# Input statistics on ScalarE, negative scales on GpSimd: a macaron block with two FP4-quantised feed-forward layers

## The chip, the cores and the metric

The kernel runs on one core of one Trainium2 chip. The metric is the device time of one execution in microseconds (us); lower is better. All arithmetic between the engines is synchronised by semaphores that the kernel places by hand, so each engine works through its own list of instructions in a fixed order and stops at a wait until another engine has counted far enough.

## The reference

```python
def _ffn(x):                       # x: (4096, 256); w_gate, w_up: (704, 256); w_down: (256, 704)
    gate = fp4_linear(x, w_gate)   # both operands quantised in blocks of 16 along the last dim
    y = fp4_linear(x, w_up)
    return fp4_linear(silu(gate) * y, w_down)

def fp4_quant_dequant(x):          # per block of 16
    scale = maximum(max(abs(xb)) / 6, 1e-12)
    q = GRID[searchsorted(MID, abs(xb / scale))] * sign(xb / scale) * scale

x = x + 0.5 * _ffn(layernorm(x))
x = x + attention(layernorm(x))    # complex projections, 2 batches of 2048 rows, width 256
x = x + 0.5 * _ffn(layernorm(x))
```

`layernorm` is (x - mean) / sqrt(var + 1e-5) over 256 columns, without gain or bias. Everything is float32.

## The kernel before

The 4096 rows of x are 32 tiles (NT = 32) of 128 rows, kept in on-chip memory as `x[:, t, :]`. Three stages follow each other: the first feed-forward layer (f = 0), attention, and the second feed-forward layer (f = 1). The change touches the two feed-forward stages alone.

A feed-forward stage is a software pipeline written out by hand. Each engine has a function `step(c, par)` and runs it for c up to 33; in step c the engines work on several tiles at once:

- TensorE transposes the quantised row of tile c (eight 128x128 transposes, `bank<-ident,zq`), computes gate and up of tile c + 3 (`gate_up`, in three column parts; the first waits for `gu_read`, that is, until VectorE has read the gate and up of the tile before), and projects tile c down (`bank_b<-wd_hl`).
- ScalarE copies the transposes out (`T_hi`), takes the SiLU of tile c + 3, normalises tile c + 7 into the last 256 columns of `z` (`normalise`, waits `yx_done`), takes absolute values of the scaled row, and copies the down projection out (`down`). In the first stage it also takes the statistics of the new x of tile c - 2 for attention: sum (L1298), minus mean twice (L1304, L1305), variance (L1311).
- VectorE multiplies SiLU by up (`product`, L776), takes the maximum of each block of 16 (`amax`, L787) of one whole row `z` of 960 columns (704 of tile c + 3 in the next step, and 256 normalised columns of a later tile), makes `s_up` (L790), `s_neg` (L794) and the reciprocal `s_inv` (L799), rounds (`rounded`, `grid`), and from tile 4 on makes the low part of the transposes (`T_lo`, L870).
- GpSimd adds the down projection of tile c - 1 to x (`residual`, L544), scales the row of tile c + 2 by `s_inv` (`y`, L552; waits `rnd_done`), and multiplies the grid of tile c + 1 by `s_neg` (`zq`, L568).

`whole(f, k)` is true for the tiles whose row GpSimd scales in one piece: k = 2 to 27 in the first stage, 3 to 27 in the second. For k from 28 on VectorE scales 704 columns itself (`scaled`, L827).

The statistics of the input (mean and variance of the 32 tiles of x as they come in) are made by ScalarE for tiles 0 to 7 ahead of the loop. For tiles 8 to 31 VectorE makes them with `bn_stats` and `bn_aggr`: two tiles in each step with c % 4 == 2, two more in each step with c % 4 == 3, there with four `bn_aggr` and two small operations for the group. Groups 3 to 7 (tiles 12 to 31) fall into steps 2 to 19 of the first stage. `group_std` on GpSimd turns a group's variances into 1/std in each step with c % 4 == 0.

```python
def step(c, par):                                   # VectorE
    blocks_of(c, par)                               # scales(c + 2), to_grid(c + 1), lower(c)
    if f == 0 and c >= 0:
        input_statistics(c)
    if hidden(c + 3):
        product(c + 3)
```

Of the kernel before, what the change touches and what calls it, by code (L numbers as in the profile page):

```python
# [15 lines left out]
SIX = 6.0  # L16
# [14 lines left out]
def macaron_kernel(nc, x_in, wq, bq, wk, bk, wv, bv, wo, bo, w_gate, w_up, w_down, out):  # L31
# [35 lines left out]
    with ctx:  # L67
# [140 lines left out]
        gate_done = sem("gate_done")  # L208
        amax_done, up_done, inv_done = sem("amax_done"), sem("up_done"), sem("inv_done")
        y_done, yx_done, abs_done = sem("y_done"), sem("yx_done"), sem("abs_done")  # L210
        rnd_done, grid_done, zq_done = sem("rnd_done"), sem("grid_done"), sem("zq_done")
# [66 lines left out]
        def wait_scaled(engine, f, k):  # L278

            if hidden(k) and not whole(f, k):  # L280
                engine.wait_ge(y_done, scaled_apart(f, k))
            if ahead(k):
                engine.wait_ge(yx_done, NT * f + k + LEAD + 1)

        def last(k):
# [158 lines left out]
        def _(pool):  # L444
# [22 lines left out]
            def group_std(g):  # L467

                q = slice(4 * g, 4 * g + 4)
                if g < 2:  # L470
                    pool.wait_ge(x_var, 4 * (g + 1))
                    nc.gpsimd.tensor_tensor(out=var[:, q], in0=var[:, q], in1=eps_all[:, q],
                                            op=ALU.add).then_inc(x_eps, 1)
                    pool.wait_ge(x_eps, g + 1)
                else:
                    pool.wait_ge(g_stats, 2 * (g - 1))
                nc.gpsimd.tensor_tensor(out=rstd[:, q], in0=var[:, q], in1=mhalf[:, q],
# [62 lines left out]
            def ffn_step(f):  # L540
                def residual(t, par):
# [3 lines left out]
                                            op=ALU.add).then_inc(x_new, 1)  # L545

                def scaled_by_pool(k):

# [7 lines left out]
                def quantised(k, par):  # L556

                    pool.wait_ge(grid_done, number(f, k))
                    if f or between(k, 1 - LEAD, NT - 1):
                        pool.wait_ge(T_done, number(f, k) - 1)  # L560
# [11 lines left out]

                def step(c, par):
                    if hidden(c - 1) and c < NT:
                        residual(c - 1, 1 - par)
# [115 lines left out]
        def _(dve):  # L691
# [77 lines left out]
            def ffn_step(f):  # L769
# [9 lines left out]
                def scales(k, par):  # L779
# [5 lines left out]
                    if lo == 0:  # L785
                        dve.wait_ge(gu_read, NT * f + k + 1)
                    nc.vector.tensor_reduce(out=amax[:, n], in_=blocks(z[:, lo:hi]), axis=AX_X, op=ALU.max,  # L787
                                            apply_absolute_value=True).then_inc(amax_done, 1)
                    dve.wait_ge(amax_done, number(f, k))
                    nc.vector.scalar_tensor_tensor(out=s_up[:, n], in0=amax[:, n], scalar=TINY * SIX,  # L790
                                                   in1=c_up[:, n], op0=ALU.max, op1=ALU.mult).then_inc(up_done, 1)
                    if f or between(k, 2 - LEAD, NT - 1):
                        dve.wait_ge(zq_done, number(f, k) - 2)
                    nc.vector.scalar_tensor_tensor(out=s_neg[:, par, n], in0=amax[:, n], scalar=TINY * SIX,  # L794
                                                   in1=c_neg[:, n], op0=ALU.max, op1=ALU.mult)
                    dve.wait_ge(up_done, number(f, k))
# [57 lines left out]
                def input_statistics(c):  # L854

                    g = (c + 10) // 4
                    if c % 4 == 2 and g < NT // 4:
                        tile_statistics(4 * g)
                        tile_statistics(4 * g + 1)
                    if c % 4 == 3 and g < NT // 4:  # L860
                        tile_statistics(4 * g + 2)
                        tile_statistics(4 * g + 3)
                        group_statistics(g)

# [41 lines left out]
                def step(c, par):  # L906
                    blocks_of(c, par)
                    if f == 0 and c >= 0:
                        input_statistics(c)
                    if hidden(c + 3):  # L910
# [286 lines left out]
        def _(act):  # L1197
# [90 lines left out]
            def bias_rows():  # L1288
# [3 lines left out]
                nc.scalar.activation(bias_row[:], bv_sum, ACT.Copy).then_inc(aw["rows_s"], 1)  # L1292

            def mean_of(t, n):

                if n:
                    act.wait_ge(stats_done, n)
                nc.scalar.activation(st_junk[:, 0, :], x[:, t, :], ACT.Identity,  # L1298
                                     accum_out=total[:, bass.ds(t, 1)]).then_inc(total_done, 1)
# [49 lines left out]
            def ffn_step(f):  # L1349
# [69 lines left out]
                def step(c, par):  # L1419
                    measured = f == 0 and 0 <= c - 2 < NT - 2  # L1420
                    extra = f == 0
                    if chain(c + 1) and (f or not last(c + 1)) and (f or c != -1):
# [11 lines left out]
                    if measured:  # L1434
                        act.wait_ge(x_new, c - 1)
                        mean_of(c - 2, c - 2)
                    if c < 0:
                        silu_gate(c + 3)
# [8 lines left out]
                    if measured:  # L1447
                        minus_mean(c - 2, c - 2)
                    if c >= 0 and hidden(c + 3):
                        silu_gate(c + 3)  # L1450
# [15 lines left out]
                    if measured:  # L1466
                        variance_of(c - 2, c - 2)
                    if f and 2 <= c < 2 + 2 * QT:
                        new_statistics(NT - 2 * QT + c - 2)
# [807 lines left out]
```

## Time and profile before

| what | value |
|---|---|
| median of 3 runs | 918.5 us (918.35 to 918.93) |
| the profiled execution: its time, its span | 917.84 us, 916.0 us |
| busy share: PE, VectorE (DVE), ScalarE (ACT), GpSimd (POOL) | 97%, 78%, 66%, 58% |
| granted TensorE clock over the span | 1.00 |

Stages by the trace: weights and first tiles to about 49 us, steps 0 to 31 of the first feed-forward layer 49 to 264 us, attention to about 704 us, steps 0 to 31 of the second layer 704 to 916 us. Busy time of a whole stage says little about what ends a wait there: in the two feed-forward stages TensorE and VectorE are both above 93% busy (209.8 and 202.5 of 215.1 us; 204.7 and 201.5 of 212.0 us), in attention TensorE has 438.1 of 440.0 us and VectorE 265.6.

### The profile page before, as it was taken

How to read it: one execution, taken by the hardware profiler on the slowest of the kernel's cores; microseconds unless marked ns; L12 is line 12 of the kernel's file. 1: busy time of each engine (PE TensorE's matmuls, PEld its weight loads, DVE VectorE, ACT ScalarE, POOL GpSimd, SP SyncE). 2: the span in 40 equal slices, each digit the busy share in tenths (PEclk: the TensorE clock that was granted, in tenths of full speed). 3: DMA queues.
4: the chain of work that ended last, by engine and by line, in shares of the span. 5: the costliest groups of instructions: out<-in, count | busy, mean ns of one | idle time of the engine just before them, and what ended most of it. 6: DMA issues, size and time to landing. Idle time of an engine off the chain costs nothing.

```text
span 916.0 us, 16066 instructions
## 1 busy us (share of the span) xinstructions
PE 888.2 (97%) x5608; PEld 796.9 (87%) x5608; DVE 711.8 (78%) x1189; ACT 601.6 (66%) x1263; POOL 528.4 (58%) x562
## 2 busy tenths in 40 slices
PE   4999999999999999999999999999999999999997
PEld 3789889889988898989998898988988899999986
DVE  7979999999976666665573644545599999999998
ACT  6777667767674675758675576767784666555543
POOL 5577778777520254545663154546577667777662
PEclk9999999999999999999999999999999999999999
DMA  9100000000000000000000000000000000000001
GB/s 317 60 1 1 1 1 2 1 1 1 1 2 0 1 2 1 1 1 1 1 1 1 1 1 1 1 1 1 1 1 1 1 25 24 24 24 24 24 1 47
DMA packets 11951, 13.80 MB, mean 15 GB/s; under 512 B 864, under 2 KB 11104, under 8 KB 11872
## 3 DMA queue, kind: packets, MB, share of 16 engines
q1 hardware_dynamic: 11872, 12.79, 4.2%
q8 instruction: 45, 0.74, 0.3%
q14 instruction: 34, 0.28, 0.1%
HBM read 8.59 MB, written 4.19 MB: 14 GB/s over the span
## 4 chain that ended last, share of the span: by engine, by line
PE 64%; DVE 26%; issue 5%; POOL 3%; ACT 1%; DMA 0%; SPq 0%; DVEq 0%; POOLq 0%; ACTq 0%
PE bank L2085 19%; PE bank L1831 12%; PE bank L2123 5%; PE bank L2127 4%; PE bank L2125 4%; DVE amax L787 4%; DVE grid L814 4%; DVE rounded L808 4%; PE bank L1712 4%; DVE z L776 4%; PE bank_b L1842 3%; DVE T_lo L870 3%; PE bank L2048 2%; PE bank_b L1849 2%; POOL p_lo L615 2%
## 5 line engine op out<-in xcount | busy, mean ns | idle before, releaser
L615 POOL TENSOR_TENSOR p_lo<-s_ring,p_hi 128x512 fp32r<-128x512 f32 x128 | 167.4, 1313 | 218.0 <-ACT p_hi L1570 217.9
L982 DVE TENSOR_TENSOR top<-bank,top 128x512 f32<-128x512 f32 x112 | 77.4, 691 | 125.7 <-ACT s_ring L1554 125.7
L1831 PE MATMUL bank<-w_hi,T_hi 128*128 128x512 f32 (+1 forms) x384 | 150.4, 392 | 5.7 <-DVE z L776 5.5
L568 POOL TENSOR_TENSOR zq<-grid,s_neg 128x256 f32<-128x256 f32 (+2 forms) x184 | 141.9, 798 | 17.7 <-DVE grid L814 17.7
L552 POOL TENSOR_TENSOR y<-z,s_inv 128x960 f32<-128x960 f32 (+1 forms) x56 | 98.4, 1757 | 83.8 <-DVE rounded L808 79.0
L1831 PE MATMUL bank<-w_hi,T_lo 128*128 128x512 f32 (+1 forms) x384 | 143.8, 374 | 0.0
L1831 PE MATMUL bank<-w_lo,T_hi 128*128 128x512 f32 (+1 forms) x384 | 143.4, 373 | 0.0
L1382 ACT ACTIVATE T_hi<-bank 128x1024 fp32r<-128x1024 f32 (+1 forms) x68 | 64.6, 951 | 105.1 <-PE bank L1712 105.1
L1554 ACT ACTIVATE s_ring<-bank 128x512 f32<-128x512 f32 x128 | 75.9, 593 | 78.0 <-PE bank L2085 77.9
L2123 PE MATMUL bank<-v_hl,p_hi 128*128 128x258 f32 x384 | 109.9, 286 | 0.4 <-DVE x L1014 0.2
L2127 PE MATMUL bank<-v_hl,p_lo 128*128 128x258 f32 x384 | 108.2, 282 | 0.0
L2125 PE MATMUL bank<-v_hl,p_hi 128*128 128x256 f32 x384 | 108.1, 282 | 0.0
L2085 PE MATMUL bank<-q_hi,k_hi 128*128 128x512 f32 x256 | 101.2, 395 | 0.8
L2085 PE MATMUL bank<-q_lo,k_hi 128*128 128x512 f32 x256 | 100.6, 393 | 0.0
L2085 PE MATMUL bank<-q_hi,k_lo 128*128 128x512 f32 x256 | 100.2, 392 | 0.0
L1560 ACT ACTIVATE s_ring<-s_ring 128x512 f32<-128x512 f32 x128 | 79.2, 622 | 18.5 <-DVE s_ring L1004 18.5
L1831 PEld LDWEIGHTS bank<-w_hi,T_hi 128*128 128x128 f32 x384 | 72.2, 188 | 17.3 <-issue 6.9
L1004 DVE TENSOR_TENSOR s_ring<-s_ring,bank 128x512 f32<-128x512 f32 x128 | 84.8, 678 | 1.3 <-PE bank L1712 0.8
L1570 ACT ACTIVATE p_hi<-s_ring 128x512 fp32r<-128x512 f32 x128 | 80.7, 632 | 7.1 <-PE bank_b L2127 3.5
L1831 PEld LDWEIGHTS bank<-w_hi,T_lo 128*128 128x128 f32 x384 | 72.1, 188 | 10.9
L1842 PE MATMUL bank_b<-wd_hl,T_hi 128*128 128x256 f32 x600 | 80.4, 279 | 0.1
L787 DVE TENSOR_REDUCE amax<-z 128x60 f32<-128x960 f32 (+2 forms) x72 | 74.9, 1040 | 7.0 <-ACT z L1416 2.0
(232 smaller groups left out, 2204.2 us busy)
## 6 DMA issues: line engine op xcount, KB each, us to landing
out<-x SPq DMA_DIRECT2D x7, 512.0 KB, 2.9
x<-in_L_attn_hidden_states SPq DMA_DIRECT2D x3, 1024.0 KB, 12.3
x<-in_L_attn_hidden_states SPq DMA_DIRECT2D x2, 512.0 KB, 6.9
wraw<-in_L_ffn_w_down SPq DMA_DIRECT2D x1, 704.0 KB, 7.3
wraw<-in_L_ffn_w_up SPq DMA_DIRECT2D x1, 640.0 KB, 4.8
wq_s<-in_L_attn_Wq SPq DMA_DIRECT2D x1, 512.0 KB, 6.4
wk_s<-in_L_attn_Wk SPq DMA_DIRECT2D x1, 512.0 KB, 7.3
wo_s<-in_L_attn_Wo SPq DMA_DIRECT2D x1, 512.0 KB, 8.2
```

Source lines behind the costliest of these rows:

```text
L552: nc.gpsimd.tensor_tensor(out=blocks(y[:, lo:Z]), in0=blocks(z[:, lo:Z]), in1=spread(s_inv[:, lo // BLOCK:ZB], (Z - lo) // BLOCK), op=ALU. ...
L568: last = nc.gpsimd.tensor_tensor(out=blocks(zq[:, to:to + hi - lo]), in0=blocks(grid[:, lo:hi]), in1=spread(s_neg[:, par, lo // BLOCK:hi / ...
L615: nc.gpsimd.tensor_tensor(out=lower_buf(n, c), in0=score_buf(n, c), in1=upper_buf(n, c).bitcast(F32), op=ALU.subtract).then_inc(plo_done, 1)
L787: nc.vector.tensor_reduce(out=amax[:, n], in_=blocks(z[:, lo:hi]), axis=AX_X, op=ALU.max, apply_absolute_value=True).then_inc(amax_done, 1)
L1004: nc.vector.tensor_tensor(out=p, in0=p, in1=shift_bank, op=ALU.subtract).then_inc(diff_done, 1)
L1570: nc.scalar.activation(upper_buf(n, c), score_buf(n, c), ACT.Copy).then_inc(phi_done, 1)
L1831: last = nc.tensor.matmul(gu[:, lo:hi], lhsT=T[:, par, HK + kd, :], rhs=w[:, kd, lo:hi], start=n == 0, stop=n == len(terms) - 1)
L1842: nc.tensor.matmul(dn, lhsT=T_hi[:, par, k, :], rhs=wd_hl[:, k, half:half + D], start=n == 0, stop=False)
L2085: last = nc.tensor.matmul(score_bank(c), lhsT=kk[:, kd, t], rhs=q[:, kd, :], start=i == 0, stop=i == len(terms) - 1)
L2123: nc.tensor.matmul(o[:, 0:D + 2], lhsT=hi[:, q], rhs=v_hl[:, c, 0:D + 2], start=c == 0, stop=False, skip_group_check=True)
L2125: nc.tensor.matmul(o[:, 0:D], lhsT=hi[:, q], rhs=v_hl[:, c, D + 2:], start=False, stop=False, skip_group_check=True)
L2127: last = nc.tensor.matmul(o[:, 0:D + 2], lhsT=lo[:, q], rhs=v_hl[:, c, 0:D + 2], start=False, stop=c == CH - 1, skip_group_check=True)
```

## The change

1. Statistics of tiles 12 to 31 move from VectorE to ScalarE: in each step 0 to 19 of the first stage ScalarE takes the sum, minus mean and variance of tile c + 12, one tile a step. GpSimd adds epsilon to a group's variances itself (`group_std` for g other than 2).
2. For tiles with `whole(f, k)` the negative scale `s_neg` is made by GpSimd (`negative_scales`), at the head of its step and behind a wait for `inv_done`, VectorE's reciprocals of tile c + 2. Since an engine works in order, the residual add of tile c - 1 now stands behind that wait too.
3. VectorE's `amax` waits for `neg_done` of the tile before, since it overwrites what GpSimd reads.

```diff
             def group_std(g):
                 q = slice(4 * g, 4 * g + 4)
-                if g < 2:
-                    pool.wait_ge(x_var, 4 * (g + 1))
+                if g != 2:
+                    pool.wait_ge(x_var, input_variances(4 * g + 3))
                     nc.gpsimd.tensor_tensor(out=var[:, q], in0=var[:, q], in1=eps_all[:, q],
                                             op=ALU.add).then_inc(x_eps, 1)
...
+                def negative_scales(k, par):
+                    pool.wait_ge(amax_done, number(f, k))
+                    pool.wait_ge(zq_done, number(f, k) - 2)
+                    nc.gpsimd.tensor_scalar(out=s_neg[:, par, :], in0=amax[:], scalar1=TINY * SIX, scalar2=-1.0 / SIX,
+                                            op0=ALU.max, op1=ALU.mult).then_inc(neg_done, 1)
...
                 def quantised(k, par):
                     pool.wait_ge(grid_done, number(f, k))
+                    if whole(f, k):
+                        pool.wait_ge(neg_done, negatives(f, k))
...
                 def step(c, par):
+                    if whole(f, c + 2):
+                        pool.wait_ge(inv_done, number(f, c + 2))
+                        negative_scales(c + 2, par)
                     if hidden(c - 1) and c < NT:
                         residual(c - 1, 1 - par)
...
+                    if k and whole(f, k - 1):
+                        dve.wait_ge(neg_done, negatives(f, k - 1))
                     nc.vector.tensor_reduce(out=amax[:, n], in_=blocks(z[:, lo:hi]), axis=AX_X, op=ALU.max,
                                             apply_absolute_value=True).then_inc(amax_done, 1)
...
-                    nc.vector.scalar_tensor_tensor(out=s_neg[:, par, n], in0=amax[:, n], scalar=TINY * SIX,
-                                                   in1=c_neg[:, n], op0=ALU.max, op1=ALU.mult)
+                    if not whole(f, k):
+                        if f or between(k, 2 - LEAD, NT - 1):
+                            dve.wait_ge(zq_done, number(f, k) - 2)
+                        nc.vector.scalar_tensor_tensor(out=s_neg[:, par, n], in0=amax[:, n], scalar=TINY * SIX,
+                                                       in1=c_neg[:, n], op0=ALU.max, op1=ALU.mult)
...
                 def step(c, par):
                     blocks_of(c, par)
-                    if f == 0 and c >= 0:
-                        input_statistics(c)
...
+            def input_sum(t):
+                if t % 8 == 0 or t == 12:
+                    act.wait_ge(x_in_s[t // 8 + 1], 16)
+                act.wait_ge(x_var, input_variances(t) - 1)
+                nc.scalar.activation(xjunk[:, 2, :], x[:, t, :], ACT.Identity,
+                                     accum_out=total[:, t:t + 1]).then_inc(x_tot, 1)
+            def minus_input_mean(t):
+                act.wait_ge(x_tot, input_variances(t))
+                nc.scalar.activation(nmean[:, t:t + 1], total[:, t:t + 1], ACT.Copy, scale=-1.0 / D)
+                nc.scalar.activation(nmean_s[:, t:t + 1], total[:, t:t + 1], ACT.Copy,
+                                     scale=-1.0 / D / ROOT).then_inc(x_nm, 1)
+            def input_variance(t):
+                act.wait_ge(x_nm, 2 + t - 11)
+                nc.scalar.activation(xjunk[:, 3, :], x[:, t, :], ACT.Square, scale=1.0 / ROOT,
+                                     bias=nmean_s[:, t:t + 1], accum_out=var[:, t:t + 1]).then_inc(x_var, 1)
...
+                    arriving = f == 0 and 12 <= c + 12 < NT
...
                     if measured:
                         act.wait_ge(x_new, c - 1)
                         mean_of(c - 2, c - 2)
+                    if arriving:
+                        input_sum(c + 12)
...
                     if measured:
                         minus_mean(c - 2, c - 2)
+                    if arriving:
+                        minus_input_mean(c + 12)
...
                     if measured:
                         variance_of(c - 2, c - 2)
+                    if arriving:
+                        input_variance(c + 12)
```

VectorE's list in step 7 of the first stage, before (a step with the statistics of two tiles and of a group; `T_lo` is the low part of the transposes of tile 7):

```order
L808 SCALAR_TENSOR_TENSOR rounded<-bank,y 128x960 [waits abs_done,yx_done]
L814 SCALAR_TENSOR_TENSOR grid<-bank,rounded 128x960 [waits zq_done,rnd_done]
L870 TENSOR_TENSOR T_lo<-bank,T_hi 128x896 [waits hi_done]
L872 TENSOR_TENSOR T_hi<-bank,T_hi 64x128
L696 BN_STATS stats<-x 128x6 x2
L704 BN_AGGR mv<-stats 128x2 [waits stat_set]
L704 BN_AGGR mv<-stats 128x2 x3
L706 TENSOR_SCALAR nmean<-mv 128x4 [waits mv_done]
L708 TENSOR_SCALAR var<-mv 128x4
L776 TENSOR_TENSOR z<-bank,silu 128x704 [waits yx_done,gu_done,silu_done]
```

The same place after the change, with the head of the next step, whose line numbers are those of the changed kernel:

```order
L833 SCALAR_TENSOR_TENSOR rounded<-bank,y 128x960 [waits abs_done,yx_done]
L839 SCALAR_TENSOR_TENSOR grid<-bank,rounded 128x960 [waits zq_done,rnd_done]
L894 TENSOR_TENSOR T_lo<-bank,T_hi 128x896 [waits hi_done]
L896 TENSOR_TENSOR T_hi<-bank,T_hi 64x128
L798 TENSOR_TENSOR z<-bank,silu 128x704 [waits yx_done,gu_done,silu_done]
L811 TENSOR_REDUCE amax<-z 128x60 [waits neg_done,gu_read,xn_done]
L814 SCALAR_TENSOR_TENSOR s_up<-amax,c_up 128x60 [waits amax_done]
L824 RECIPROCAL s_inv<-s_up 128x60 [waits yx_done,up_done]
```

The nine statistics instructions and `s_neg` have left VectorE's list, and `amax` has one wait more.

ScalarE's list over one step of the first stage (from step 4 to 13), before:

```order
L1371 ACTIVATE down<-bank_b 128x256 [waits x_new,dn_done]
L1298 ACTIVATE st_junk,total<-x 128x256 [waits stats_done,x_new]
L1382 ACTIVATE T_hi<-bank 128x1024 [waits T_done]
L1304 ACTIVATE nmean<-total 128x1 [waits total_done]
L1305 ACTIVATE nmean_s<-total 128x1
L1406 ACTIVATE silu<-bank 128x704 [waits gu_read,gate_done]
L1311 ACTIVATE st_junk,var<-x,nmean_s 128x256 [waits nmean_done]
L1416 ACTIVATE z<-x,nmr,rstd 128x256 [waits yx_done,g_nmr]
```

And now:

```order
L1414 ACTIVATE down<-bank_b 128x256 [waits x_new,dn_done]
L1341 ACTIVATE st_junk,total<-x 128x256 [waits stats_done,x_new]
L1321 ACTIVATE xjunk,total<-x 128x256 [waits x_var]
L1425 ACTIVATE T_hi<-bank 128x1024 [waits T_done]
L1347 ACTIVATE nmean<-total 128x1 [waits total_done]
L1348 ACTIVATE nmean_s<-total 128x1
L1327 ACTIVATE nmean<-total 128x1 [waits x_tot]
L1328 ACTIVATE nmean_s<-total 128x1
L1449 ACTIVATE silu<-bank 128x704 [waits gu_read,gate_done]
L1354 ACTIVATE st_junk,var<-x,nmean_s 128x256 [waits nmean_done]
L1334 ACTIVATE xjunk,var<-x,nmean_s 128x256 [waits x_nm]
L1459 ACTIVATE z<-x,nmr,rstd 128x256 [waits yx_done,g_nmr]
```

A sum stands ahead of the copy `T_hi`, and two short operations and a variance stand ahead of the normalised columns `z`, for which VectorE's next `amax` waits.

GpSimd's list over a step with `group_std`, before:

```order
L568 TENSOR_TENSOR zq<-grid,s_neg 128x64
L477 TENSOR_TENSOR rstd<-var,mhalf 128x4 [waits g_stats]
L480 TENSOR_TENSOR nmr<-nmean,rstd 128x4 [waits g_rstd]
L544 TENSOR_TENSOR x<-x,down 128x256 [waits down_done]
L552 TENSOR_TENSOR y<-z,s_inv 128x960 [waits rnd_done,inv_done]
```

And now:

```order
L587 TENSOR_TENSOR zq<-grid,s_neg 128x64
L482 TENSOR_TENSOR var<-var,eps_all 128x4 [waits x_var]
L487 TENSOR_TENSOR rstd<-var,mhalf 128x4 [waits x_eps]
L490 TENSOR_TENSOR nmr<-nmean,rstd 128x4 [waits g_rstd]
L561 TENSOR_SCALAR s_neg<-amax 128x60 [waits zq_done,amax_done,inv_done]
L554 TENSOR_TENSOR x<-x,down 128x256 [waits down_done]
L569 TENSOR_TENSOR y<-z,s_inv 128x960 [waits rnd_done,inv_done]
```

The residual add `x`, which was ready as soon as `down` was, now stands behind `s_neg` and its wait for the reciprocals.

## Rows read from the trace of the kernel before

**Rows 1.** The page: busy time of each engine over the span.

```profile
PE 888.2 (97%) x5608; PEld 796.9 (87%) x5608; DVE 711.8 (78%) x1189; ACT 601.6 (66%) x1263; POOL 528.4 (58%) x562
```

**Rows 2.** Windows from tile to tile: start:end, length, busy by engine (x instructions).

```profile
92.13:192.03 99.90, 95.44 (x603) 86.22 (x602) 96.35 (x166) 66.84 (x160) 74.70 (x87) 1.00 0.00 1
218.75:246.06 27.31, 27.31 (x174) 24.78 (x172) 26.58 (x41) 18.43 (x45) 17.40 (x21) 1.00 0.00 1
732.74:780.59 47.85, 47.85 (x303) 43.41 (x302) 46.24 (x64) 32.05 (x71) 35.07 (x39) 1.00 0.07 23
780.59:874.28 93.69, 93.69 (x604) 85.84 (x602) 90.66 (x127) 50.88 (x70) 67.86 (x73) 1.00 0.07 23
880.97:895.29 14.32, 13.94 (x88) 12.44 (x87) 13.96 (x23) 5.76 (x8) 6.51 (x8) 1.00 0.00 0
```

**Rows 3.** Timeline of TensorE in the first stage: start, length, operation [idle before].

```profile
133.88 0.47 PE L1831 MATMUL bank<-w_hi,T_hi 128*128 128x512 f32 x1 [1.09 <-DVE z L776]
...
142.04 1.03 PE L1712 MATMUL bank<-ident,zq 128*128 128x128 f32 x8
...
145.34 1.34 PE L1842 MATMUL bank_b<-wd_hl,T_hi 128*128 128x256 f32 x10
...
147.34 0.40 PE L1831 MATMUL bank<-w_hi,T_hi 128*128 128x512 f32 x1
...
148.72 1.04 PE L1712 MATMUL bank<-ident,zq 128*128 128x128 f32 x8
```

**Rows 4.** Timeline of VectorE over the same steps.

```profile
131.34 0.75 DVE L696 BATCH_NORM_STATS2 stats<-x 128x6 f32<-128x256 f32 x2
...
132.85 0.89 DVE L776 TENSOR_TENSOR z<-bank,silu 128x704 f32<-128x704 f32 x1
...
140.35 1.15 DVE L787 TENSOR_REDUCE amax<-z 128x60 f32<-128x960 f32 x1
141.54 0.22 DVE L790 SCALAR_TENSOR_TENSOR s_up<-amax,c_up 128x60 f32<-128x60 f32 x1
141.68 0.21 DVE L794 SCALAR_TENSOR_TENSOR s_neg<-amax,c_neg 128x60 f32<-128x60 f32 x1
141.81 0.52 DVE L799 RECIPROCAL s_inv<-s_up 128x60 f32<-128x60 f32 x1
...
146.86 1.15 DVE L787 TENSOR_REDUCE amax<-z 128x60 f32<-128x960 f32 x1
```

**Rows 5.** Timeline of ScalarE in step 13.

```profile
143.12 1.03 ACT L1382 ACTIVATE T_hi<-bank 128x1024 fp32r<-128x1024 f32 x1 [1.48 <-PE bank L1712]
144.04 0.19 ACT L1304 ACTIVATE nmean<-total 128x1 f32<-128x1 f32 x1
...
144.50 0.76 ACT L1406 ACTIVATE silu<-bank 128x704 f32<-128x704 f32 x1 [0.17 <-PE bank L1831]
145.15 0.50 ACT L1311 ACTIVATE st_junk<-x,nmean_s 128x256 f32<-128x256 f32 x1
...
145.64 0.59 ACT L1416 ACTIVATE z<-x,nmr,rstd 128x256 f32<-128x256 f32 x1
```

**Rows 6.** Timeline of GpSimd, steps 13 and 14.

```profile
145.28 2.22 POOL L568 TENSOR_TENSOR zq<-grid,s_neg 128x256 f32<-128x256 f32 x3
...
149.00 0.73 POOL L544 TENSOR_TENSOR x<-x,down 128x256 f32<-128x256 f32 x1
150.00 1.83 POOL L552 TENSOR_TENSOR y<-z,s_inv 128x960 f32<-128x960 f32 x1 [0.27 <-DVE rounded L808]
```

**Rows 7.** Timelines of VectorE and GpSimd in the second stage, one step.

```profile
746.15 0.68 DVE L790 SCALAR_TENSOR_TENSOR s_up<-amax,c_up 128x60 f32<-128x60 f32 x1
...
746.01 0.74 POOL L544 TENSOR_TENSOR x<-x,down 128x256 f32<-128x256 f32 x1 [0.41 <-ACT down L1371]
```

**Rows 8.** GpSimd's groups by form: shapes, count, busy us, mean ns, idle.

```profile
L568 POOL TENSOR_TENSOR zq<-grid,s_neg 128x64 f32<-128x64 f32 x60 | 18.6, 310 | 0.0
...
L637 POOL TENSOR_SCALAR xn<-x,nmean,rstd 128x256 f32<-128x256 f32 x8 | 4.3, 556 | 0.8 <-PE bank L1708 0.8
```

More of the change, by code:

```diff
@@ L209, in macaron_kernel @@
         amax_done, up_done, inv_done = sem("amax_done"), sem("up_done"), sem("inv_done")
+        neg_done = sem("neg_done")
         y_done, yx_done, abs_done = sem("y_done"), sem("yx_done"), sem("abs_done")
@@ L283, in wait_scaled, with input_variances, negatives @@
                 engine.wait_ge(yx_done, NT * f + k + LEAD + 1)
+        def input_variances(t):
+            return t + 1 if t < 8 else t - 3
+        def negatives(f, k):
+            before = sum(whole(0, j) for j in range(NT)) if f else 0
+            return before + sum(whole(f, j) for j in range(k + 1))
         def last(k):
@@ L469, in group_std @@
                 q = slice(4 * g, 4 * g + 4)
-                if g < 2:
-                    pool.wait_ge(x_var, 4 * (g + 1))
+                if g != 2:
+                    pool.wait_ge(x_var, input_variances(4 * g + 3))
                     nc.gpsimd.tensor_tensor(out=var[:, q], in0=var[:, q], in1=eps_all[:, q],
                                             op=ALU.add).then_inc(x_eps, 1)
-                    pool.wait_ge(x_eps, g + 1)
+                    pool.wait_ge(x_eps, g + 1 if g < 2 else g)
                 else:
-                    pool.wait_ge(g_stats, 2 * (g - 1))
+                    pool.wait_ge(g_stats, 2)
                 nc.gpsimd.tensor_tensor(out=rstd[:, q], in0=var[:, q], in1=mhalf[:, q],
@@ L791, in scales @@
                                                    in1=c_up[:, n], op0=ALU.max, op1=ALU.mult).then_inc(up_done, 1)
-                    if f or between(k, 2 - LEAD, NT - 1):
-                        dve.wait_ge(zq_done, number(f, k) - 2)
-                    nc.vector.scalar_tensor_tensor(out=s_neg[:, par, n], in0=amax[:, n], scalar=TINY * SIX,
-                                                   in1=c_neg[:, n], op0=ALU.max, op1=ALU.mult)
+                    if not whole(f, k):
[3 more added lines that the diff above has]
+                                                       in1=c_neg[:, n], op0=ALU.max, op1=ALU.mult)
                     dve.wait_ge(up_done, number(f, k))
@@ L854, in input_statistics @@
                 def input_statistics(c):
[L856 to L863, printed above, removed]
+                    if c == -2:
+                        tile_statistics(8)
+                        tile_statistics(9)
+                    if c == -1:
+                        tile_statistics(10)
+                        tile_statistics(11)
+                        group_statistics(2)
                 def lower(k, par):
```

## Prediction, made before the changed kernel ran

> **What bounds the kernel now.** The page comes first: TensorE is busy for 97% of the span [rows 1], but its ends are modelled, so I read in the timelines what a step costs it. A step is the distance between the transposes of two tiles: 142.04 to 148.72, 6.68 us, with no stop [rows 3]. That is TensorE's own work, and the floor of every step from tile 4 to 27.
>
> VectorE's own step is the distance between two `amax` without statistics, 140.35 to 146.86, 6.51 us, without a gap [rows 4]. It is just shorter than TensorE's, so whatever is added comes out of a margin of 0.17. The statistics take 131.34 to 132.85, 1.51 us, in a step c % 4 == 3 [rows 4], and half of it or so (two `bn_stats`, 0.75 and a gap: 0.78) in the step before. Over four steps VectorE needs 4 x 6.51 + 1.51 + 0.78 = 28.33 us, TensorE 4 x 6.68 = 26.72. The difference is seen as TensorE standing 1.09 us for VectorE's `z` at 133.88 [rows 3]. So in steps 2 to 19 of the first stage VectorE is the bound, and elsewhere in the feed-forward stages TensorE, with VectorE close behind.
>
> The windows then give each stretch of whole steps [rows 2]; all begin and end with a tile's transposes. Against 6.68 a step:
> - first stage, tiles 6 to 20: 99.90 for 14 steps, 6.38 too long
> - first stage, tiles 24 to 28: 27.31 for 4, 0.59 too long
> - second stage, tiles 4 to 11: 47.85 for 7, 1.09 too long
> - second stage, 11 to 25: 93.69 for 14, 0.17 too long
> - second stage, 26 to 28: 14.32 for 2, 0.96 too long
>
> Attention is not touched.
>
> **A. The statistics leave VectorE.** Five groups of 1.51 + 0.78 are 11.5 us of VectorE time. Not all was on the path: what TensorE lost is the 6.38 of the first window. With VectorE at 6.51 or less and TensorE at 6.68 the path gets back 6.38, if ScalarE keeps up.
>
> **ScalarE's cover.** A step adds a sum, two short operations and a variance. The variance costs 0.49 (145.15 to 145.64), the sum is the same shape and costs no more, two short operations took 144.04 to 144.50 less 0.17 idle, 0.29 [rows 5]. That is at most 1.27 a step. The sum falls into the 1.48 us for which `T_hi` waits for TensorE [rows 5]. The short ones fill the 0.17 and push SiLU by 0.12 at most; the variance pushes `z` by 0.49. So `z`, which ended at 145.64 + 0.59 = 146.23, ends between 146.7 and 146.85 (0.8 later at the very most: 147.0), and `amax` came at 146.86 [rows 4]: it starts about where it did, at worst near 147.05. Followed on: VectorE's product starts 5.51 behind `amax` (a step of 6.51 less the 0.99 to 1.00 from 132.85 to 133.84, which is 131.34 + 1.51 + the product), ends 0.89 later, and TensorE goes 0.14 behind it (132.85 + 0.89 to 133.88). That is 147.05 + 6.54 = 153.6, and TensorE wants it one step after 147.34, at 154.02 [rows 3]. The margin is 0.4 us. What is late next, `T_hi`, has 1.48 before it, less 0.49 for the sum and 0.6 for what was pushed: still not late. I cost the added work at nothing; without that cover it is 1.27 x 20 = 25 us.
>
> **B. `s_neg` leaves VectorE.** It has 0.21 us of its own, but the reciprocal behind it must wait for `s_up` anyway, which ends 0.22 after its start: `s_up` 141.54, `s_inv` 141.81 [rows 4]. Without `s_neg` the reciprocal could start at about 141.79. The bounds are 0.02 and 0.13 (the distance from `s_neg` to `s_inv`); I take 0.02 a step. The added wait on `neg_done` is satisfied long before, but may cost VectorE a few hundredths. These two cancel.
>
> **C. The residual add moves behind the reciprocals.** In the second stage `s_up` takes 0.68 us instead of 0.22: it starts at 746.15, GpSimd's residual add runs 746.01 to 746.75, and `s_up` ends at 746.83, 0.08 behind it [rows 7]. So the two do not run together; `s_up` loses up to 0.46. This is why VectorE, 6.51 on its own, keeps TensorE waiting a little wherever the add falls there, and has no lead left when tile 28 comes, from which VectorE's steps are longer (it scales 704 columns itself). Behind the reciprocals the add meets `rounded`. That happened already in the steps with 1/std: the add at 149.00 ran behind `s_inv`, which began at 148.32 (146.86 + 1.46), took its 0.73, and did no harm that shows [rows 4, 6]. Then VectorE has about 0.17 a step in hand. I take back all four smaller windows: 0.59 + 1.09 + 0.17 + 0.96 = 2.81, and 0.3 for the ends of the two stages, where VectorE leads. Bounds: nothing, and 2.81 + 1.5 if the whole lead, one `s_up` delay in each of three last steps, reaches the end.
>
> The Trainium skill ("SBUF — State Buffer", section Who interferes with whom) says that a VectorE instruction with two SBUF inputs excludes a GpSimd instruction that reads SBUF, whichever starts first, and that one with a PSUM input does not. The trace agrees: `s_up` has two, `rounded` one. By the rule the sum is the same 2.81, and anything GpSimd does between `amax` and `s_inv` would bring the loss back.
>
> **D. GpSimd's new order.** The price of `s_neg` there is not in the trace. Nearest from below: a product of 64 columns, 0.31; from above: the two-step operation on 256 columns, 0.56 [rows 8]. 60 columns are nearer the first: 0.31. In the tightest steps, with 1/std: `zq` ends at 147.50, the 1/std work runs to 149.00, the reciprocals end at 148.84 (146.86 + 1.46 + 0.52), the add takes 0.73 and `y` starts at 150.00 with 0.27 idle [rows 4, 6]. With 0.31 in front `y` starts at 150.04, with 0.56 at 150.3. In the other steps everything waits for 148.84 plus some 0.12, and comes out the same. `y` late by 0.3 makes `zq` of the next tile end at 154.4, and TensorE transposes it at 155.4: hidden.
>
> **The sum.** 6.38 + 2.81 + 0.3 = 9.5 us. The profiled execution took 917.84 for a span of 916.0, 0.66 below the median; so 908.3 for its like, and 918.5 - 9.5 = **909.0 us** against the median, 1.0% less.
>
> **Rivals.**
> 1. *Only A comes.* The smaller windows have another cause, or the lead is eaten by new waits of VectorE (for `z` from ScalarE, for `neg_done`). Speaks for it: the margin is only 0.17 a step. Against: the 0.08 between the ends in rows 7. Gain 6.4: 912.1 us. Chance 0.15.
> 2. *ScalarE becomes the bound of steps 0 to 19.* If the new work pushes `z` by 1 us more than the 0.8, the loop from `T_hi` over `z`, `amax` and product back to TensorE, which spans two steps, is 0.6 too long, 0.3 a step, 6 us over 20 steps: gain 3.5, 915.0 us. For it: steps 0 to 3, where ScalarE also makes `T_lo`, have the least room, but they cost TensorE more too. Against: all four durations stand in rows 5. Chance 0.06.
> 3. *GpSimd becomes the bound, and it is slower than before.* The loop runs reciprocals, `s_neg`, add, `y`, product, `amax`, reciprocals: 0.12 + n + 0.73 + 1.83 + 0.14 + 0.99 + 1.46 + 0.52 = 5.79 + n, and passes 6.68 when `s_neg` costs n = 0.9. From 1.1 on, over the 51 tiles concerned, it eats the 9.5. At 1.3 it is 0.4 x 51 = 20 us less 9.5: 929 us. Against: it needs over twice the 0.56. Chance 0.03.
> 4. *The change gives nothing*, since another wait at once takes the place of VectorE's. The steps of 6.68 that lie between the statistics say no. Chance 0.01.
>
> The forecast has 0.75.
>
> **How the numbers follow.** 918.5 less 10.7 (A, and C with its upper bound) is 907.8; with 0.3 for the spread of the runs shown the lower end is 907.5. The upper end takes in rival 1: 912.5. About 0.1 to 0.2 is left out. Some 0.2% of the time is what a measurement of this kernel tells from no change. Faster: forecast, rivals 1 and 2, with something off for what I have not seen: 0.94; same 0.02; slower 0.04.
>
> **What would show it.** Steps of 6.68 to 6.70 between all transposes of tiles 5 to 28 in both stages, and no stop of TensorE for VectorE's `z` (A). `s_up` at 0.22 in the second stage, against 0.4 to 0.7 (C). `s_neg` on GpSimd near 0.3 and `y` starting right behind `rounded` (D). VectorE idle, by 0.1 to 0.2 a step, before `z` or `amax`. ScalarE's idle time before `T_hi` down from 1.48 to 0.5. The prediction is wrong if `amax` waits for ScalarE's `z` by more than 0.4 us a step, or if `s_up` goes on being held.

## The result and the profile after

| what | before, run beside it | changed |
|---|---|---|
| median | 918.71 us (918.35 to 919.49, 4 runs) | 908.1 us (907.7 to 908.92, 4 runs) |
| ratio to before, 95% interval | | 0.9884, 0.9871 to 0.9897 |
| the profiled execution: its time, its span | 917.84, 916.0 us | 908.92, 907.1 us |

The change takes 10.6 us off, 1.16%. The forecast was 909.0 us, with a range of 907.5 to 912.5. Times in this document are in us where no unit stands.

The page of the changed kernel, busy time of each engine, answers to [rows 1]:

```profile
PE 884.5 (98%) x5608; PEld 796.5 (88%) x5608; DVE 693.5 (76%) x1088; ACT 620.5 (68%) x1383; POOL 548.2 (60%) x618
```

VectorE has lost 18.3 us, ScalarE and GpSimd have gained 18.9 and 19.8. The engines together work more than before and the kernel is shorter. TensorE's busy time went down by 3.7 without a change to its list, so the figure of before held some waiting: in [rows 2] it is busy for all 27.31 us of tiles 24 to 28, a stretch that is 0.59 too long. The next view is the windows of the changed kernel from tile to tile; the stretches are those of [rows 2].

```profile
93.64:187.17 93.53, 93.53 (x603) 85.77 (x602) 88.25 (x114) 80.71 (x242) 81.02 (x104) 1.00 0.01 1
213.89:240.61 26.72, 26.72 (x173) 24.50 (x172) 25.79 (x38) 18.35 (x45) 18.83 (x23) 1.00 0.00 1
726.94:773.70 46.76, 46.76 (x303) 42.87 (x301) 43.98 (x57) 32.06 (x71) 37.31 (x45) 1.00 0.07 24
773.70:867.22 93.52, 93.52 (x604) 85.74 (x602) 89.11 (x114) 49.55 (x70) 73.20 (x88) 1.00 0.07 23
873.90:887.26 13.36, 13.36 (x88) 12.25 (x86) 13.00 (x21) 5.65 (x8) 6.49 (x8) 1.00 0.00 1
```

Against [rows 2] they are 6.37, 0.59, 1.09, 0.17 and 0.96 shorter, and each is now a whole number of steps of 6.68. The stage ends gave 0.43 (tile 28 of the first stage to attention's first matmul, 17.83 to 17.40) and 0.87 (tile 28 of the second to the end of the span, 20.71 to 19.84). From the first transposes of tile 0 to the end that is 10.2 us, with 0.25 lost in steps 0 to 5 and 0.1 in attention. The profiled span is only 8.9 shorter, since tile 0 began at 51.10 instead of 49.84. That is spread: e5 below, whose start is the changed kernel's, has it at 49.83.

TensorE over the steps of [rows 3], timeline of the changed kernel (start, length, operation):

```profile
133.73 1.04 PE L1762 MATMUL bank<-ident,zq 128*128 128x128 f32 x8
...
140.41 1.04 PE L1762 MATMUL bank<-ident,zq 128*128 128x128 f32 x8
...
145.71 0.40 PE L1881 MATMUL bank<-w_hi,T_hi 128*128 128x512 f32 x1
...
147.09 1.04 PE L1762 MATMUL bank<-ident,zq 128*128 128x128 f32 x8
```

The transposes come every 6.68 us, and no matmul has idle time in brackets; in [rows 3] the first of `gate_up` had 1.09 for VectorE's `z`. VectorE over one step:

```profile
137.30 0.89 DVE L798 TENSOR_TENSOR z<-bank,silu 128x704 f32<-128x704 f32 x1
138.45 1.15 DVE L811 TENSOR_REDUCE amax<-z 128x60 f32<-128x960 f32 x1 [0.26 <-ACT z L1459]
139.64 0.22 DVE L814 SCALAR_TENSOR_TENSOR s_up<-amax,c_up 128x60 f32<-128x60 f32 x1
139.90 0.53 DVE L824 RECIPROCAL s_inv<-s_up 128x60 f32<-128x60 f32 x1
...
143.98 0.89 DVE L798 TENSOR_TENSOR z<-bank,silu 128x704 f32<-128x704 f32 x1
```

VectorE now waits, 0.26 a step, for ScalarE's `z`, which comes later than before. That costs nothing: the product at 143.98 is done at 144.87 and TensorE takes it up at 145.71. From `s_up` to `s_inv` it is 0.26; in [rows 4], with `s_neg` between them, it was 0.27. ScalarE in the same step:

```profile
133.23 0.41 ACT L1321 ACTIVATE xjunk<-x 128x256 f32<-128x256 f32 x1
133.53 0.19 ACT L1321 ACTIVATION_READ_ACCUMULATOR xjunk<-x 128x1 f32 x1
134.81 1.03 ACT L1425 ACTIVATE T_hi<-bank 128x1024 fp32r<-128x1024 f32 x1 [1.08 <-PE bank L1762]
...
135.91 0.19 ACT L1327 ACTIVATE nmean<-total 128x1 f32<-128x1 f32 x1
136.01 0.19 ACT L1328 ACTIVATE nmean_s<-total 128x1 f32<-128x1 f32 x1
136.19 0.76 ACT L1449 ACTIVATE silu<-bank 128x704 f32<-128x704 f32 x1
...
137.33 0.50 ACT L1334 ACTIVATE xjunk<-x,nmean_s 128x256 f32<-128x256 f32 x1
137.73 0.19 ACT L1334 ACTIVATION_READ_ACCUMULATOR xjunk<-x,nmean_s 128x1 f32 x1
137.82 0.59 ACT L1459 ACTIVATE z<-x,nmr,rstd 128x256 f32<-128x256 f32 x1
```

The variance takes 0.49 (137.33 to 137.82), as [rows 5] had it; the sum takes 0.40, since `T_hi`'s wait went from 1.48 to 1.08; the two short operations take 0.18 and fill the 0.17 for which SiLU had waited. GpSimd in a step with 1/std and the next:

```profile
133.82 0.41 POOL L561 TENSOR_SCALAR s_neg<-amax 128x60 f32<-128x60 f32 x1 [1.35 <-DVE s_inv L824]
134.32 0.74 POOL L554 TENSOR_TENSOR x<-x,down 128x256 f32<-128x256 f32 x1
135.01 1.83 POOL L569 TENSOR_TENSOR y<-z,s_inv 128x960 f32<-128x960 f32 x1
...
138.98 0.20 POOL L482 TENSOR_TENSOR var<-var,eps_all 128x4 f32<-128x4 f32 x1
139.26 1.03 POOL L487 TENSOR_TENSOR rstd<-var,mhalf 128x4 f32<-128x4 f32 x1
...
140.65 0.42 POOL L561 TENSOR_SCALAR s_neg<-amax 128x60 f32<-128x60 f32 x1
141.15 0.74 POOL L554 TENSOR_TENSOR x<-x,down 128x256 f32<-128x256 f32 x1
141.84 1.83 POOL L569 TENSOR_TENSOR y<-z,s_inv 128x960 f32<-128x960 f32 x1
```

`s_neg` takes 0.41 and 0.50 from start to start, not 0.31. With 1/std GpSimd's own list is 6.83 us long (135.01 to 141.84), longer than TensorE's step; the 1.35 of idle time in other steps makes up for it. Two steps in every four have such work, one for a group of the input and one for a group of the new x. The view of waits of the changed kernel, 100 to 187 us (total us, times, longest), shows that little of this reaches VectorE:

```profile
ACT T_hi L1425 <- PE bank L1762: 11.7, 13, 1.1
POOL s_neg L561 <- DVE s_inv L824: 8.4, 7, 1.5
DVE amax L811 <- ACT z L1459: 2.3, 10, 0.3
DVE z L798 <- POOL y L569: 0.3, 1, 0.3
```

### The profile page after: what moved, and what is told of

It reads as the page before. It is cut to its first block, busy times and chain, and to the rows that moved or that the text cites. A ratio compares the mean times of both kernels' runs of the same rounds, so it can differ in the third digit from the quotient of the medians.

```text
span 907.1 us, 16197 instructions
## 1 busy us (share of the span) xinstructions
PE 884.5 (98%) x5608; PEld 796.5 (88%) x5608; DVE 693.5 (76%) x1088; ACT 620.5 (68%) x1383; POOL 548.2 (60%) x618
## 4 chain that ended last, share of the span: by engine, by line
PE 88%; DVE 5%; ACT 2%; issue 2%; POOL 2%; DMA 1%; SPq 0%; DVEq 0%; POOLq 0%; ACTq 0%
PE bank L1881 24%; PE bank L2135 19%; PE bank_b L1892 7%; PE bank L1762 7%; PE bank_b L1899 5%; PE bank L2175 4%; PE bank L2177 4%; PE bank L2173 4%; PE bank L2098 2%; PE bank_b L2177 1%; PE bank_b L2173 1%; PE bank_b L2175 1%; PE bank L2116 1%; PE bank_b L2116 1%; DMA wk_s<-in_L_attn_Wk 1%
## 5 line engine op out<-in xcount | busy, mean ns | idle before, releaser
L1881 PEld LDWEIGHTS bank<-w_hi,T_lo 128*128 128x128 f32 x384 | 72.2, 188 | 10.6
```

The costliest lines, as they stand in the source:

```text
L1881: last = nc.tensor.matmul(gu[:, lo:hi], lhsT=T[:, par, HK + kd, :], rhs=w[:, kd, lo:hi], start=n == 0, stop=n == len(terms) - 1)
```

## The experiments

All times of before are those of its runs on the same chip: 918.39 us (9 runs) for the first four, 918.52 (15) for the next four, 919.08 (7) for the last three. Medians are over 4 or 5 runs unless said.

**One part alone.** In e1 only the statistics move: `s_neg` and the add are as before.

```diff
 def step(c, par):                     # GpSimd, changed kernel
-    if whole(f, c + 2):
-        pool.wait_ge(inv_done, number(f, c + 2))
-        negative_scales(c + 2, par)
     if hidden(c - 1) and c < NT:
         residual(c - 1, 1 - par)
...                                    # VectorE makes s_neg again
```

> The statistics of tiles 12 to 31 on ScalarE alone; the negative scales stay on VectorE and GpSimd adds to x ahead of them, as before. My theory (6.4 us from the statistics, the rest from the add that moved behind the reciprocals): 6.4 us under the kernel before, about 912.3; the window of 14 steps from tile 6 to 20 is 93.5 us, s_up still takes 0.4 us or more in the mean in the second stage, and the window from tile 4 to 11 there stays near 47.8. Rival (the statistics give it all): 908 to 909, with the second stage short too.

Measured: 911.43 us (910.97 to 912.15), ratio 0.9922 (0.9909 to 0.9934). Its windows of the first stage, tiles 6 to 20 and 24 to 28:

```profile
92.95:186.55 93.60, 93.60 (x604) 85.78 (x603) 89.91 (x128) 80.72 (x242) 75.15 (x91) 1.00 0.00 1
213.30:240.05 26.75, 26.75 (x174) 24.52 (x173) 25.88 (x39) 18.36 (x45) 17.35 (x20) 1.00 0.00 1
```

The first line is A. The second is the surprise: the prediction had put these 0.59 us on C, and they came without it; so did the 0.4 of the stage's end. The second stage stayed as it was (7.44 and 6.81 at tiles 26 to 28, mean `s_up` 387 ns).

In e2 all but the statistics is changed; they stay on VectorE.

```diff
-arriving = f == 0 and 12 <= c + 12 < NT
+arriving = False                      # ScalarE
     blocks_of(c, par)                 # VectorE
+    if f == 0 and c >= 0:
+        input_statistics(c)
...
```

> The complement: negative scales on GpSimd and the add behind the reciprocals, statistics left on VectorE. My theory: 2.8 plus 1 us under the kernel before, about 915 (914.5 to 916); the 14 steps from tile 6 to 20 stay at 99 us or more, the second stage has steps of 6.68 throughout. Rival (the statistics give it all): 918.7, no change. Rival (GpSimd's longer list costs when VectorE leads nowhere): 920 or more.

Measured: 914.7 us (914.45 to 915.14), ratio 0.9958 (0.9945 to 0.997). The second stage has steps of 6.68 throughout and the short end. But tiles 24 to 28 of the first stage are at 6.68 here too, so e1 and e2 both gain them: 6.96 + 3.69 = 10.65 us, where 1.0 counted twice should leave 9.65 for the whole. It is 10.2 to 10.6. Of the 0.5 to 1.0 between, 0.3 is seen: tiles 6 to 20 take 100.12 in e2 against 99.90 before (its four long steps with statistics are 8.11 to 8.13), and 93.60 in e1 against 93.53, which the whole change does not pay. The rest is no larger than the spread of the runs.

Why e1 gains those 0.59 can be read in the kernel before. Its VectorE was still catching up after the last statistics when it met the add, shortly ahead of the transposes of tile 23:

```profile
211.25 0.22 DVE L790 SCALAR_TENSOR_TENSOR s_up<-amax,c_up 128x60 f32<-128x60 f32 x1
211.35 0.73 POOL L544 TENSOR_TENSOR x<-x,down 128x256 f32<-128x256 f32 x1 [0.65 <-ACT down L1371]
211.39 0.77 DVE L794 SCALAR_TENSOR_TENSOR s_neg<-amax,c_neg 128x60 f32<-128x60 f32 x1
```

Here `s_up` came first and took its 0.22, but `s_neg`, 0.04 behind the start of the add, was held: 0.77 instead of 0.21, until 0.08 behind the add. The reciprocal came 0.56 later for it (0.83 behind the start of `s_up`, not 0.27), and in the next two steps the add was ahead of `s_up`, which took 0.53 and 0.51. In e1 VectorE is further ahead there: at 212.33 and 219.00 both operations are free.

**Which of the two moves does C's work.** In e3 the add stands behind the reciprocals, but VectorE keeps `s_neg`.

```diff
     if whole(f, c + 2):
         pool.wait_ge(inv_done, number(f, c + 2))
-        negative_scales(c + 2, par)
     residual(c - 1, 1 - par)
...                                    # VectorE makes s_neg again
```

> Statistics on ScalarE, and the add behind the wait for the reciprocals, but the negative scales made by VectorE as before. My theory (s_neg was hidden behind the latency of s_up, 0.02 us a step): the same as the changed kernel, 908.1 within 0.5. Rival (VectorE's shorter list matters, 0.13 to 0.21 us a step): 910 or more.

Measured: 908.22 us (907.86 to 908.78), ratio 0.9887 (0.9874 to 0.9901). That is the changed kernel's time. Giving `s_neg` to GpSimd is worth nothing once the add stands behind the reciprocals.

In e4 GpSimd makes `s_neg`, but adds first.

```diff
+    residual(c - 1, 1 - par)
     if whole(f, c + 2):
         pool.wait_ge(inv_done, number(f, c + 2))
         negative_scales(c + 2, par)
-    residual(c - 1, 1 - par)
```

> Statistics on ScalarE and negative scales on GpSimd, but the add to x ahead of them, free to start as soon as down is there. My theory (the add meets s_up and holds it): s_up at 0.4 us or more in the mean in the second stage, no gain there, 911.5 to 912.5. Rival (it is the shorter list of VectorE that gives the lead): 908 to 909 as in the changed kernel, since s_neg is gone from VectorE here too.

Measured: 910.21 us (910.09 to 910.27), ratio 0.9909 (0.9894 to 0.9924): better than expected, with most steps at 6.67 to 6.70, but 7.50 and 6.82 at tiles 26 to 28 of the second stage. One step of it there, VectorE and GpSimd:

```profile
846.16 0.43 DVE L814 SCALAR_TENSOR_TENSOR s_up<-amax,c_up 128x60 f32<-128x60 f32 x1
...
845.76 0.74 POOL L554 TENSOR_TENSOR x<-x,down 128x256 f32<-128x256 f32 x1
```

`s_up` is still held until 0.09 behind the add. The collision remains, and costs 2 us. It is not there in every step of the second stage: but for one case (0.60 at 712.22) `s_up` is at 0.22 up to 765.80, then held at 772.29 and 785.73 and from 792.64 on in each step. In most of the steps before, `s_up` starts only 0.02 ahead of the add and is free, and it is the add that takes longer, 0.79 instead of 0.73 (745.76 and 745.78).

The 1.2 us by which e4 beats e1, which differs from it in `s_neg` alone, have a cause in the traces. In e1, as before, VectorE still makes `s_neg`, and where the add starts 0.02 behind `s_up` it holds `s_neg` instead: 0.75 at 726.12 and at 760.28. Both times some steps with a held `s_up` follow. The steps of e1 between tiles 4 and 10 are up to 6.98 long, those of e4 at most 6.69. So `s_neg` is worth something on GpSimd as long as the add is free, and nothing behind the reciprocals.

**ScalarE's margin.** e5 and e6 add one and three more variances of the same tile to each step, which write to scratch memory that nobody reads.

```diff
 def input_variance(t):
     act.wait_ge(x_nm, 2 + t - 11)
+    nc.scalar.activation(xjunk[:, 1, :], x[:, t, :], ACT.Square, scale=1.0 / ROOT,
+                         bias=nmean_s[:, t:t + 1])        # e6: three times
```

> The changed kernel with one more variance-shaped ScalarE operation of about 0.40 us ahead of z in each of the steps 0 to 19 (its result goes to a scratch area). In the trace of the changed kernel VectorE's product ends at 144.87 in a step where TensorE wants it at 145.71, 0.7 us of margin. My theory: the 0.4 is swallowed in steps 4 to 19, steps 0 to 3 grow by up to 0.25 each; 908.3 to 909.3. Rival (ScalarE is already the bound): 0.2 to 0.4 us a step, 912 to 916.

Measured: 908.33 us (908.24 to 909.35), ratio 0.9891 (0.9874 to 0.9907). 0.40 us more in each of 20 steps is hidden, but for 0.5 in steps 3 to 6: from tile 0 to 7 it takes 49.70, the changed kernel 49.23.

> The same with three more such operations, 1.2 us a step. My theory: 0.5 us over the margin, paid once in two steps, 0.25 a step over 16 steps, and 1.0 in each of the steps 0 to 3: 8 us over the changed kernel, 913 to 918. Rival (no margin): 1.2 x 20 = 24 us, 932. Rival (still hidden): 908 to 909.

Measured: 915.64 us (915.32 to 916.19), ratio 0.9969 (0.9954 to 0.9984). Its timeline of TensorE's transposes:

```profile
123.14 1.04 PE L1768 MATMUL bank<-ident,zq 128*128 128x128 f32 x8
...
130.39 1.03 PE L1768 MATMUL bank<-ident,zq 128*128 128x128 f32 x8
...
137.08 1.03 PE L1768 MATMUL bank<-ident,zq 128*128 128x128 f32 x8
...
144.33 0.93 PE L1768 MATMUL bank<-ident,zq 128*128 128x128 f32 x7
```

Steps of 7.25 and 6.69 take turns: a loop that spans two steps is 13.94 long instead of 13.36. The four steps from tile 17 to 21 are 7.05 each. In its view of waits, 100 to 187 us, VectorE's `amax` stands for ScalarE's `z`:

```profile
DVE amax L811 <- ACT z L1465: 7.5, 12, 1.0
```

**GpSimd's margin.** e7 and e8 make the negative scales two and four times; the extra ones go to scratch memory.

```diff
 def negative_scales(k, par):
     ...
+    nc.gpsimd.tensor_scalar(out=st_junk[:, 1, 0:60], in0=amax[:], scalar1=TINY * SIX,
+                            scalar2=-1.0 / SIX, op0=ALU.max, op1=ALU.mult)    # e8: three times
     nc.gpsimd.tensor_scalar(out=s_neg[:, par, :], in0=amax[:], ...)
```

> The changed kernel with a second s_neg operation on GpSimd (into a scratch area) ahead of the first, 0.5 us a step more. The prediction's loop passes 6.68 us at 0.9 for all of s_neg; here it is 1.0, so 0.1 x 51 = 5 us over the changed kernel; the steps with 1/std on GpSimd have no room to catch up and can double that: 911 to 918. Rival (GpSimd is off the path, its row is long finished): 908.1.

Measured: 919.34 us (918.99 to 920.69, 10 runs), ratio 1.0009 (1.0 to 1.0019). 0.49 us more a step takes back all that the change gave, though 5.79 + 0.99 is only 0.1 over a step. Its timeline of GpSimd's `y`:

```profile
102.98 1.84 POOL L571 TENSOR_TENSOR y<-z,s_inv 128x960 f32<-128x960 f32 x1
...
109.65 1.83 POOL L571 TENSOR_TENSOR y<-z,s_inv 128x960 f32<-128x960 f32 x1
...
116.97 1.84 POOL L571 TENSOR_TENSOR y<-z,s_inv 128x960 f32<-128x960 f32 x1
```

A step without 1/std is 6.67 long, one with it 7.32, which is 6.83 + 0.49. VectorE's product then waits for `y` (6.4 in 12 waits, 100 to 187 us), and the second stage ends as before (7.54 and 6.82), its lead gone. TensorE has ten steps of 7.28 to 7.34 in the first stage and three of 7.3 in the second, 8.1 us in all; most of the other 3 is at the ends of the two stages.

> Three more s_neg operations, 1.5 us a step more, 2.0 in all. By the loop 1.1 us a step over 51 tiles, 56 us, so about 960 to 975. Rival (the loop is longer than I reckon, and GpSimd has room): under 930.

Measured: 965.05 us (965.03 to 965.06, 2 runs), ratio 1.0505 (1.0484 to 1.0526). Steps are 7.60 to 7.63, with 1/std 8.25 to 8.28. The view of waits, 100 to 200 us:

```profile
DVE z L804 <- POOL y L575: 19.3, 13, 1.8
```

This is the loop of rival 3: VectorE's product stands for `y` in every step. Four scales at 0.49 to 0.50 are 2.0 us, so the loop of 7.61 is 5.6 + n, against the 5.79 + n of the prediction.

**Does the add's place matter once VectorE leads?** e13 is e3 with the add free again from step 13 of the second stage on.

```diff
-    if whole(f, c + 2):
+    if whole(f, c + 2) and not (f and c > 12):
         pool.wait_ge(inv_done, number(f, c + 2))
     residual(c - 1, 1 - par)
```

> Statistics on ScalarE, negative scales on VectorE, add behind the reciprocals in the first stage and in steps 1 to 12 of the second; from step 13 on the add is free again, as before. Theory of the lead: the add and s_up meet only when VectorE is late; with VectorE ahead, s_up comes first, is not held, and the lead keeps itself: s_up stays at 0.22 to the end, 908.2, steps of 6.68 through tile 28. Rival (the add meets s_up wherever it is free to): s_up back to 0.4 from step 13, 6.69 to 6.70 a step, 7.5 in the step from tile 26 to 27, 909.5 to 910.

Measured: 908.17 us (907.7 to 908.53), ratio 0.9884 (0.9869 to 0.9899). One late step, VectorE and GpSimd of e13:

```profile
845.01 0.22 DVE L801 SCALAR_TENSOR_TENSOR s_up<-amax,c_up 128x60 f32<-128x60 f32 x1
...
845.22 0.75 POOL L553 TENSOR_TENSOR x<-x,down 128x256 f32<-128x256 f32 x1 [0.92 <-ACT down L1400]
```

The same place in e1, whose lists there are the same:

```profile
840.83 0.41 DVE L799 SCALAR_TENSOR_TENSOR s_up<-amax,c_up 128x60 f32<-128x60 f32 x1
...
840.43 0.73 POOL L553 TENSOR_TENSOR x<-x,down 128x256 f32<-128x256 f32 x1 [0.15 <-ACT down L1398]
```

In e13 VectorE is through with `s_up` when the add becomes ready; in e1 the add comes 0.4 ahead of it. Call VectorE's lead the time from `s_up` to TensorE's next transposes: it is 0.93 in e13 and 0.32 in e1. Same instructions, same waits: only this lead differs, and from step 13 to the end of the stage it keeps itself.

**Is it the second operand?** e10 is e4 with `s_up` made by an instruction with a single tensor operand.

```diff
-nc.vector.scalar_tensor_tensor(out=s_up[:, n], in0=amax[:, n], scalar=TINY * SIX,
-                               in1=c_up[:, n], op0=ALU.max, op1=ALU.mult)
+nc.vector.tensor_scalar(out=s_up[:, n], in0=amax[:, n], scalar1=TINY * SIX, scalar2=INV_SIX_UP,
+                        op0=ALU.max, op1=ALU.mult)
```

> The kernel with the add ahead of the negative scales (910.2), with s_up made by the form that has one tensor input and two constants in place of a second tensor. Theory A (only an operation with two tensor inputs from SBUF is held): s_up is never held, no s_up over 0.3 in the second stage, about 908.2. Theory B (this form is held too when it starts during the add): some s_up above 0.5, the second stage as before, about 910.2.

Measured: 909.54 us (909.44 to 909.82), ratio 0.99 (0.9885 to 0.9915), with 7.48 at tile 26. VectorE and GpSimd in one step:

```profile
852.31 0.41 DVE L814 TENSOR_SCALAR s_up<-amax 128x60 f32<-128x60 f32 x1
...
851.93 0.73 POOL L554 TENSOR_TENSOR x<-x,down 128x256 f32<-128x256 f32 x1 [0.15 <-ACT down L1414]
```

It takes 0.19 when it is free and is held all the same, to 0.06 behind the add. One operand does not help.

**The cost in the first steps.** In e11 tiles 12 to 15 keep their statistics on VectorE, in steps 2 and 3, where ScalarE has the least room.

```diff
-arriving = f == 0 and 12 <= c + 12 < NT
+arriving = f == 0 and 16 <= c + 12 < NT
+if c == 2: tile_statistics(12); tile_statistics(13)                        # VectorE
+if c == 3: tile_statistics(14); tile_statistics(15); group_statistics(3)
...
```

> The changed kernel with the statistics of tiles 12 to 15 left on VectorE in steps 2 and 3, ScalarE from tile 16 on. Steps 0 to 3 have 7.16 us, in which VectorE stood still; the changed kernel's 7.59 and 6.81 at tiles 0 and 4 should go back to 7.45 and 6.68, 0.27 us less, about 907.8. Rival: VectorE enters tile 4 late from the two steps and loses 0.2 to 1 us from tile 6 on, 908.3 to 909.

Measured: 907.72 us (907.49 to 908.0), ratio 0.9879 (0.9863 to 0.9896). Step 0 takes 7.47 (changed kernel 7.59), step 4 6.68 (6.81). The 0.25 us is back in these steps; in the medians it can't be told from the changed kernel's 908.1, though it is the lowest of the study.

## Why the prediction was right, point by point

- **The bound.** Right. With the statistics gone from VectorE, TensorE is the bound of both feed-forward stages, in steps of 6.68.
- **A.** Right in place and size: 6.38 foreseen, 6.37 in the changed kernel. e1 has it without the rest.
- **ScalarE's cover.** Right. The added work came to 1.07 a step against at most 1.27; the prediction gave 0.4 of margin, e5 hides 0.40. Rival 2 was priced well: `z` pushed by 1.8 in all was to cost 0.3 a step. In e6 it is pushed by some 1.7 (0.49 in the changed kernel and 1.2 more), and that costs 0.29 ((7.25 + 6.69) / 2 - 6.68), 0.37 in the last four steps. What was costed at nothing and isn't is steps 0 to 4, 0.25 in all, which e11 takes back.
- **B.** Right: 0.01 a step, by e3 nothing. An independent instruction in the 0.26 for which `s_inv` waits for `s_up` is free, so taking it away gives nothing. That holds where nothing else holds `s_neg`: beside a free add it can cost VectorE 0.5 (0.77 at 211.39 before), which the prediction did not see.
- **C.** The size was right, its cause half so. Failed is the premise that the loss depends on the add's place alone. The second stage's 2.22 and its end are the add's, since e1 does not have them and e2 and e3 do. The other 0.59 of the first stage, and 0.4 at its end, are not: e1 gets them by A alone, e2 by the add alone. What both give is VectorE's lead. Before, VectorE came out of the statistics with less of it, the add held first `s_neg` and then `s_up`, and losses of up to 0.5 a step kept VectorE late. The prediction took the collision for a fixed property of where the add stands; e13 and e1 show that it is one of two states, each of which lasted over the same dozen steps, from 13 of the second stage on. Neither is safe elsewhere: in the first stage of e1 `s_up` is held four times (0.73, 0.39, 0.74 and 0.39, from 98.98 to 132.76) and never after. In the second stage the late state is entered, in e1 and before alike; e4 turns late from step 10 on. There ScalarE makes its last statistics (763.48), and `down` and the add begin 6.31 and 6.33 behind those of the step before, `s_up` only 6.49 behind: the add overtakes it. That this is what tips it is read from one trace; no run tried it, and it stays open. e13 frees the add only after that place.
- **The ends.** Mis-sized: 0.3 for both, 0.43 + 0.87 came. This is the lead at the end, which the prediction had in its upper bound. The 1.0 that was not counted, less the 0.25 lost in the first steps, is most of why the changed kernel lies 0.9 below the forecast; the other 0.15 is within the spread of the runs. That the two errors have opposite signs helped the number.
- **D.** Mis-sized without harm: `s_neg` is 0.41, 0.50 with the gap, not 0.31. The step that failed is that GpSimd's margin was read off the loop alone. Rival 3 has the change break even at n = 1.1; e7, at 0.99, is already back at the time of before (1.0009), for the steps with 1/std have no room: there GpSimd's own list is 6.83 long, 0.15 over TensorE's step already, which VectorE's lead hides; with 0.49 more it no longer does. The loop itself was near, 5.6 + n against 5.79 + n.
- **The rivals.** Rival 1 gives 912.1; e1 is that kernel, with 911.43. Rivals 2 and 3 did not occur, and e6 and e8 show what they look like. Rival 4 is out.

The Trainium skill ("SBUF — State Buffer", section Who interferes with whom) says that VectorE and GpSimd share a pair of SBUF ports, under a lock that whoever comes first keeps, and counts `tensor_scalar` among the VectorE operations that can take it too. This case agrees: `s_up` is held until 0.06 to 0.09 behind the add in e4 and e10, with the `tensor_scalar` of e10 as well, and in e13, where it comes first, it is not. The prediction went further: anything that GpSimd does between `amax` and `s_inv` would bring the loss back. In e13 the add starts there, at 845.22, and brings back nothing: `s_up` and `s_neg` have started, and the reciprocal that starts behind it (845.28) takes its usual 0.52. The page speaks of a single meeting. That the delay sets up the next meeting, and can go on for a dozen steps, is what the runs add.

## What to carry to other kernels

Two engines that exclude each other can settle in either of two orders, and the wrong one costs on every pass; a wait that fixes the order is cheap insurance, and work taken off the late engine can have the same effect, as e1 has in the first stage. Read an engine's margin from its whole list in its longest step, not only from the loop through it: here the loop left GpSimd 0.6 us and the steps with 1/std left it none. Moving a small instruction off an engine gains nothing if it lay in the gap before a dependent one, unless another engine can hold it there.

## What the hardware showed beside this

- While GpSimd's add runs, it holds whichever of VectorE's `s_up` and `s_neg` starts behind it (0.68 at 746.15 and 0.77 at 211.39, before). The reciprocal is not held (0.52 at 845.28 in e13). Where `s_up` starts first, by 0.02, the add takes 0.79 instead of 0.73 (e4).
- A one-operand VectorE instruction on 60 columns, 0.19 us alone, is held as the two-operand one is (0.41 at 852.31 in e10).
- ScalarE's sums and variances with the accumulator read cost 0.40 and 0.49 from start to start; without the read a variance costs 0.40 (e5, e6). Operations of one column cost 0.09 to 0.10 each where another of them follows (135.73 to 136.01).
- GpSimd's 60-column operation costs 0.41, though its product of 64 columns costs 0.31 [rows 8].
- The first tile's transposes began anywhere from 49.8 to 51.1 us over the profiles, also in kernels whose instructions up to there are the same (e5 49.83, the changed kernel 51.10). A single profiled span can therefore be off by 1.3 us, more than some of the terms of the sum; windows from tile to tile are not.
